# Transposing small adapter tiles on VectorE instead of TensorE in a fused residual chain

## The chip, the cores and the metric

One Trainium2 chip, one core. The time is the device time of the whole kernel in microseconds (us), from one launch. The kernel before took 558.91 us, the median of three runs (558.53 to 559.02).

## The reference

x has 64 batches of 32 channels by 512. Four layers are added to it one after the other:

```
x = x + L0(x)   # SwiGLU MLP with a low-rank adapter per batch of 32 rows
x = x + L1(x)   # 32x32 channel mixing, chosen per batch
x = x + L2(x)   # 512x512 linear plus top-2 of 8 low-rank experts
x = x + L3(x)   # 32x32 channel mixing, chosen per batch

# L0, with 16 adapters of rank 16:
t    = einsum('bri,bni->bnr', A[idx], inp)                   # 32 rows x 16
lora = base + einsum('bor,bnr->bno', B[idx], t) * 0.5
act  = silu(lora(x, gate)) * lora(x, up)                     # 512 -> 1376
down = lora(act, down)                                       # 1376 -> 512
```

The change is in L0 alone, where the small results t (for gate and up) and td (for down) must be turned so that the rank lies on the partitions before they are multiplied with B.

## The kernel before

**Tiles and steps.** The 2048 rows are 16 tiles of 128 rows, and a tile holds 4 batches. L0 works in 48 steps, ORDER (L122): three chunks of F for each tile, n = 0 (352 columns), 1 and 2 (512 each). Step s computes gate and up of its chunk, their product act, and down of the chunk two steps back. The first six steps have an order of their own, since the weights still arrive; from step 6 on step s is tile s // 3, chunk s % 3. After L0 the other layers run tile by tile. Every operand of a matmul is split into a high part in float32r and a low rest; a product is three matmuls (`product`, L1354), and where one side holds both parts stacked on the partitions, two (`stacked`, L1360).

**The adapters.** t of all four adapters of a tile is computed for all 128 rows: 128 columns, in the order batch, gate or up, rank. For n = 0 and tile 2 and later these columns are part of gate's matmuls (480 columns). A mask (`mask_t`, L1116) keeps for each row only the columns of its own batch and scales them by 0.5, so that the result is block-diagonal in batches. It writes the masked 64 columns twice (d = 0, 1), so that a 128x128 transpose on TensorE (`transpose_t`, L1401, twice, for gate and up) gives them on 128 partitions: 64 for the high part and 64 for the low one. ScalarE casts all 128 partitions (`job_hi`, kind "t", L948), and VectorE overwrites the upper 64 with the rest (`job_lo`, kind "t", L1193). The result t_hl is the stationary operand of `adapters(s)` (L1409), for all three steps of the tile. td goes the same way with one transpose: `mask_td` (L1129), `transpose_td` (L1453), kind "td", and `down_adapters` (L1457), which closes a tile's down; then "x1" adds the residual and SP stores the tile.

**The order.** ScalarE and VectorE both walk through the list `lane_jobs(s)` (L226): ScalarE does the high part of each split, VectorE the low part and the products; each waits for the other by semaphores (s_hi, s_lo), strictly in list order. After a step's jobs ScalarE also does `high_bd` (L1005), which waits for a DMA that stores an earlier block. For a tile after the third the list of n = 0 is: mask of t, act, t, gate, next b. For n = 1: act, x, bd, gate, mask of td, next b. For n = 2: td, act, x1, the next adapters' weights, gate, next b. TensorE's order is written out from L1542 on. For n = 0 it is gate, up, transpose_t, down of s - 2, adapters. For n = 2: half of gate, transpose_td, the rest of gate, half of up, down_adapters, the rest of up, adapters, down of s - 2. POOL gathers the adapters' rows with indirect DMAs; the rows of B lie in the order given by the index idx_rank, made with the mask is_rank (L102, L1101). SP's queue moves act through memory so that it lands turned: VectorE first turns act in squares of 32 by 32 within SBUF (`blocks`, L1141), which is the only use of its transpose in L0.

Of the kernel before, what the change touches and what calls it, by code (L numbers as in the profile page):

```python
# [29 lines left out]
F32 = mybir.dt.float32  # L30
# [7 lines left out]
P = 128  # L38
# [57 lines left out]
def const_array():  # L96
    p = np.arange(P)
    blocks = {

        "scale_ch": LORA_SCALE * (p[:, None] // CH == np.arange(TB)[None, :]),  # L100

        "is_rank": p[:, None] // RANK % TB == np.arange(TB)[None, :],  # L102
        "is_ch": p[:, None] // CH == np.arange(TB)[None, :],
        "row_rank": (p % RANK)[:, None],
        "row_ch": (p % CH)[:, None],
        "row": p[:, None],
        "unit_ch": p[:, None] % CH == np.arange(CH)[None, :],
        "iota": np.broadcast_to(np.arange(EXPERTS), (P, EXPERTS)),
    }
# [116 lines left out]
def lane_jobs(s):  # L226
# [38 lines left out]
def bass_conditioned_residual_chain(nc, x_t, x_rows, it_cond, it_lang, wgu, wd, a_all, a_gu, a_d, b_d,  # L265
# [6 lines left out]
    with ExitStack() as ctx:  # L272
# [59 lines left out]
        b_sel, b_raw = sb_raw("b_sel", [2, 2, 2 * H], mem_a)  # L332
        t_m = sb("t_m", [2, 2, TR], F32, mem_a)

        t_hl = sb("t_hl", [2, 2, P], F32R, mem_a)

        picked = t_m[:, 0, 0, :]
        td = sb("td", [2, TR], F32, mem_a)
        td_hl = sb("td_hl", [P], F32R, mem_a)
# [11 lines left out]
        act_t = ps("act_t", [HC, P], banks_a)  # L351
        t_ps = ps("t_ps", [HC, P], banks_a)
        banks_a.close()
# [88 lines left out]
        s_tm = sem("s_tm")  # L442
        s_tt = sem("s_tt")
        s_gu = sem("s_gu")
# [9 lines left out]
        s_tdm = sem("s_tdm")  # L454
        s_tdt = sem("s_tdt")
        s_dl = sem("s_dl")
# [110 lines left out]
        def base_cols(i):  # L567

            at = (1 - i % 2) * AD_HALF
            return down_ps[:, :, at:at + HALF]  # L570

        def td_of(i):
# [315 lines left out]
        def _(sc):  # L888
# [15 lines left out]
            def job_hi(job):  # L904
# [43 lines left out]
                elif kind == "t":  # L948
                    i = job[1]
                    sc.wait_ge(s_tt, i + 1)  # L950
                    if i >= 2:
                        sc.wait_ge(s_gu, gu_done(i - 2))
                    hi(t_hl[:, i % 2, :, :], t_ps[:, 0:2, :])
                elif kind == "td":
                    i = job[1]
                    sc.wait_ge(s_tdt, i + 1)
                    if i >= 1:
                        sc.wait_ge(s_dl, i)
                    hi(td_hl[:], t_ps[:, 2, :])
# [115 lines left out]
        def _(ve):  # L1075
# [37 lines left out]
            def lo(out_, raw, high):  # L1113
                return ve.tensor_tensor(out_, raw, high.bitcast(F32), ALU.subtract)  # L1114

            def mask_t(i):  # L1116

                ve.wait_ge(s_tx, i + 1)
                if i >= 1:
                    ve.wait_ge(s_tt, i)  # L1120
                t = t_of(i).rearrange("p (b m r) -> p m b r", m=2, r=RANK)
                for m in range(2):
                    ins = ve.tensor_tensor(
                        t_m[:, m, :, :].rearrange("p d (b r) -> p d b r", r=RANK),
                        t[:, m, :, :].unsqueeze(1).to_broadcast([P, 2, TB, RANK]),
                        const("scale_ch").unsqueeze(1).unsqueeze(3).to_broadcast([P, 2, TB, RANK]), ALU.mult)
                ins.then_inc(s_tm, 1)

            def mask_td(i):  # L1129
                ve.wait_ge(s_d, NC * (i + 1))  # L1130
                if i >= 1:
                    ve.wait_ge(s_tdt, i)
                for d in range(2):
                    ins = ve.tensor_tensor(
                        td[:, d, :].rearrange("p (j b r) -> p j b r", j=2, r=RANK),
                        td_of(i).rearrange("p j (b r) -> p j b r", r=RANK),
                        const("scale_ch").rearrange("p (j b) -> p j b", j=2).unsqueeze(3).to_broadcast(
                            [P, 2, TB // 2, RANK]), ALU.mult)
                ins.then_inc(s_tdm, 1)

# [18 lines left out]
            def job_lo(job):  # L1159
# [193 lines left out]
        def _(pe):  # L1353
# [46 lines left out]

            def transpose_t(i):  # L1401
                pe.wait_ge(s_tm, i + 1)
                if i == 0:
                    pe.wait_ge(s_ident, 16)
                for m in range(2):
                    mm = pe.transpose(t_ps[:, m, :], t_m[:, m, :, :].rearrange("p d n -> p (d n)"), ident)
                mm.then_inc(s_tt, 1)

            def adapters(s):  # L1409
# [10 lines left out]
            def transpose_act(d):  # L1420
                i, n = divmod(d, NC)
                s = step_of(i, n)
                pe.wait_ge(s_mul, s + 1)
                before = max((k for k in range(d) if k not in MOVED), default=None)
                if before is not None:
# [6 lines left out]
            def down(d):  # L1432
# [18 lines left out]
                mm.then_inc(s_d, 1)  # L1451

            def transpose_td(i):  # L1453
                pe.wait_ge(s_tdm, i + 1)
                pe.transpose(t_ps[:, 2, :], td[:].rearrange("p d n -> p (d n)"), ident).then_inc(s_tdt, 1)

# [91 lines left out]
            up(1, 0, HC // 2)  # L1548
            transpose_t(0)
            up(1, HC // 2, HC)  # L1550
# [4 lines left out]
            transpose_act(0)  # L1555
            transpose_t(1)
            whole(up, 3)
# [12 lines left out]
            gate(5, HC // 2, HC)  # L1570
            transpose_td(0)
            transpose_act(3)
# [9 lines left out]
            whole(up, 6)  # L1582
            transpose_t(2)
# [34 lines left out]
            l2_base(0, 0, 0, 1)  # L1618
            transpose_td(NT - 1)
            l1(2)  # L1620
# [94 lines left out]
```

## Time and profile before

| | |
|---|---|
| median of three runs | 558.91 us |
| time of the profiled execution | 558.51 us |
| its span, first to last instruction | 556.7 us |
| TensorE busy (matmuls) | 546.2 us, 98% |
| VectorE busy | 314.4 us, 56% |
| ScalarE busy | 210.5 us, 38% |
| POOL busy | 209.2 us, 38% |
| granted clock of TensorE | 1.00 of full speed in all slices |

Busy time is a sum over instructions, and a matmul's end is modelled and overlaps the next one's start; so the busy time of TensorE does not tell how fast it could be, and the distance between starts is the better measure of a matmul's price. Idle time of another engine costs nothing as long as TensorE doesn't wait for it.

### The profile page before, as it was taken

What the parts mean: (1) busy time and instruction counts of PE and PEld (TensorE: products, weight loads), DVE (VectorE), ACT (ScalarE), POOL (GpSimd) and SP (SyncE); (2) the same over time, 40 slices, a digit from 0 to 9 for tenths busy, and PEclk for the clock granted to TensorE, in tenths of its full rate; (3) what the DMA queues carried; (4) which work ended last, traced back from release to release, by engine and by line L of the source; (5) the groups of instructions that cost most, each with busy time, mean ns of one, the idle gap of its engine ahead of it and who ended that gap; (6) DMA issues with size and microseconds to landing.
All of it is one profiled execution on the core that took longest, in us unless ns stands there. A gap on an engine that the chain in (4) does not pass through costs nothing.

```text
span 556.7 us, 8715 instructions
## 1 busy us (share of the span) xinstructions
PE 546.2 (98%) x3172; PEld 493.2 (89%) x3172; DVE 314.4 (56%) x717; ACT 210.5 (38%) x416; POOL 209.2 (38%) x236
## 2 busy tenths in 40 slices
PE   5999999999999999999999999999999999999997
PEld 5879988898889898989898989898989899999996
DVE  6797364544464545454545454545454477777775
ACT  6675132423342424242424232323233442444442
POOL 5852144746584747332323332232322232122100
PEclk9999999999999999999999999999999999999999
DMA  8984346666666666656464645555545832676742
GB/s 289 369 252 171 114 151 207 171 205 195 197 205 203 196 210 189 206 188 192 148 190 148 183 156 185 153 182 158 179 158 175 304 97 93 195 240 211 234 145 77
DMA packets 72027, 104.68 MB, mean 188 GB/s; under 512 B 9392, under 2 KB 39728, under 8 KB 71984
## 3 DMA queue, kind: packets, MB, share of 16 engines
q1 hardware_dynamic: 60960, 66.82, 36.5%
q0 software_dynamic: 10880, 37.23, 22.3%
q8 instruction: 25, 0.41, 0.3%
q14 instruction: 18, 0.15, 0.1%
q10 hardware_dynamic: 144, 0.06, 0.1%
HBM read 77.87 MB, written 26.21 MB: 187 GB/s over the span
## 4 chain that ended last, share of the span: by engine, by line
PE 90%; DMA 5%; DVE 2%; SPq 1%; ACT 1%; issue 0%; ACTq 0%; DVEq 0%
PE gu_ps L1356 13%; PE gu_ps L1358 13%; PE gu_ps L1357 13%; PE down_ps L1356 8%; PE down_ps L1357 8%; PE down_ps L1358 8%; PE l_ps L1356 5%; PE l_ps L1357 5%; PE l_ps L1358 5%; PE gu_ps L1363 3%; PE gu_ps L1364 3%; DMA x_res<-act_blocks 1%; DMA b_sel_raw<-b_gu,idx_rank 1%; SPq L704 1%; DMA bd<-bd_hl 1%; DMA act_blocks<-act 1%
## 5 line engine op out<-in xcount | busy, mean ns | idle before, releaser
L794 POOL DMA_INDIRECT b_sel_raw<-b_gu,idx_rank x48 | 48.1, 1001 | 154.9 <-PE gu_ps L1364 144.8
L1356 PE MATMUL down_ps<-wd_sb,act_hl 128*128 128x288 f32 (+1 forms) x352 | 105.1, 299 | 0.6 <-DVE wd_sb L1114 0.3
L1357 PE MATMUL down_ps<-wd_sb,act_hl 128*128 128x288 f32 (+1 forms) x352 | 103.8, 295 | 0.0
L1358 PE MATMUL down_ps<-wd_sb,act_hl 128*128 128x288 f32 (+1 forms) x352 | 103.6, 294 | 0.0
L1356 PE MATMUL gu_ps<-w_sb,xt 128*128 128x512 f32 x256 | 102.0, 399 | 0.0
L1358 PE MATMUL gu_ps<-w_sb,xt 128*128 128x512 f32 x256 | 100.4, 392 | 0.0
L1357 PE MATMUL gu_ps<-w_sb,xt 128*128 128x512 f32 x256 | 100.3, 392 | 0.0
L794 POOL DMA_INDIRECT a_raw<-a_all,idx_batch x60 | 65.6, 1093 | 60.1 <-DVE wd_sb L1114 46.1
L1178 DVE TENSOR_TENSOR act<-act,gu_ps 128x512 f32<-128x512 f32 (+1 forms) x47 | 29.8, 634 | 98.2 <-ACT act L917 98.2
L917 ACT ACTIVATE act<-gu_ps 128x512 f32<-128x512 f32 (+1 forms) x47 | 26.1, 555 | 147.5 <-PE gu_ps L1364 147.5
L1356 PEld LDWEIGHTS down_ps<-wd_sb,act_hl 128*128 128x128 f32 (+1 forms) x352 | 66.0, 188 | 2.9 <-DVE act_hl L1114 1.0
L1357 PEld LDWEIGHTS down_ps<-wd_sb,act_hl 128*128 128x128 f32 (+1 forms) x352 | 66.1, 188 | 1.2
L1358 PEld LDWEIGHTS down_ps<-wd_sb,act_hl 128*128 128x128 f32 (+1 forms) x352 | 66.0, 188 | 0.0
L1358 PEld LDWEIGHTS gu_ps<-w_sb,xt 128*128 128x128 f32 x256 | 48.0, 188 | 10.6
L1356 PEld LDWEIGHTS gu_ps<-w_sb,xt 128*128 128x128 f32 x256 | 48.1, 188 | 9.4
L1357 PEld LDWEIGHTS gu_ps<-w_sb,xt 128*128 128x128 f32 x256 | 48.2, 188 | 8.2
L1114 DVE TENSOR_TENSOR b_sel<-b_sel_raw,b_sel 128x1024 fp32r<-128x1024 f32 (+1 forms) x48 | 52.3, 1090 | 1.3 <-ACT b_sel L897 1.2
L858 POOL TENSOR_TENSOR x_hl<-x,x_hl 128x512 fp32r<-128x512 f32 x16 | 21.6, 1353 | 69.8 <-ACT x_hl L1021 69.8
L897 ACT CAST b_sel<-b_sel_raw 128x1024 fp32r<-128x1024 f32 (+1 forms) x48 | 45.7, 953 | 1.4 <-DMA b_sel_raw<-b_gu,idx_rank 1.1
L1356 PE MATMUL l_ps<-w2ra_hl,x2t_hl 128*128 128x328 f32 (+1 forms) x128 | 41.6, 325 | 0.0
L1357 PE MATMUL l_ps<-w2ra_hl,x2t_hl 128*128 128x328 f32 (+1 forms) x128 | 39.7, 311 | 0.0
L1358 PE MATMUL l_ps<-w2ra_hl,x2t_hl 128*128 128x328 f32 (+1 forms) x128 | 39.5, 309 | 0.0
(160 smaller groups left out, 1054.5 us busy)
## 6 DMA issues: line engine op xcount, KB each, us to landing
act_blocks<-act SPq DMA_DIRECT2D x39, 256.0 KB, 4.0
x_res<-act_blocks SPq DMA_DIRECT2D x156, 64.0 KB
xt_raw<-x_t SPq DMA_DIRECT2D x16, 256.0 KB, 4.9
w_sb_raw<-wgu SPq DMA_DIRECT2D x16, 256.0 KB, 8.0
x_res<-x_rows SPq DMA_DIRECT2D x16, 256.0 KB, 2.8
x_after_l<-x_res SPq DMA_DIRECT2D x16, 256.0 KB, 2.0
bd<-bd_hl SPq DMA_DIRECT2D x16, 256.0 KB, 2.3
x<-x_after_l SPq DMA_DIRECT2D x16, 256.0 KB, 2.8
```

Source lines behind the costliest of these rows:

```text
L704: sp.dma_start(x_res[j * CH:(j + 1) * CH, 1, :].rearrange("f (b n) -> f b n", b=TB), act_scratch[d % 2, :, j * P:(j + 1) * P].rearrange("( ...
L794: nc.gpsimd.indirect_dma_start(out=dst, out_offset=None, in_=table, in_offset=bass.IndirectOffsetOnAxis(ap=idx, axis=0)).then_inc(s, 16)
L858: pool.tensor_tensor(x1_hl[:, t % 2, 1, :], x1[:, t % 2, :], x1_hl[:, t % 2, 0, :].bitcast(F32), ALU.subtract).then_inc(s_x1lo, 1)
L897: sc.copy(out_, in_).then_inc(s_hi, 1)
L917: sc.activation(act_of(s), gate_of(s), ACT.Silu).then_inc(s_silu, 1)
L1114: return ve.tensor_tensor(out_, raw, high.bitcast(F32), ALU.subtract)
L1178: ve.tensor_tensor(a, a, up_of(s), ALU.mult).then_inc(s_mul, 1)
L1356: pe.matmul(out_, stationary[0], moving[0], start=start, stop=False, skip_group_check=True)
L1357: pe.matmul(out_, stationary[0], moving[1], start=False, stop=False, skip_group_check=True)
L1358: return pe.matmul(out_, stationary[1], moving[0], start=False, stop=stop, skip_group_check=True)
L1363: pe.matmul(out_, stationary, moving[0], start=False, stop=False, skip_group_check=True)
L1364: return pe.matmul(out_, stationary, moving[1], start=False, stop=True, skip_group_check=True)
```

## The change

TensorE no longer transposes t and td. The mask writes its columns once. The high part is cast by ScalarE from the masked tile in SBUF into t_rows, with high and low side by side (batch, part, rank: 32 columns for each batch); VectorE subtracts the low part, transposes the 128 columns in squares of 32 by 32, and copies the result into t_hl. Since the masked tile is block-diagonal in squares of 32, the squares on the diagonal are the whole transpose and the others are zero. The partitions of t_hl are now in the order batch, part, rank, so the rows of B are gathered by the mask is_ch. VectorE waits for each of its own results (`turn`) before it uses it. The tile t_m is shared by t and td, and the squares of t are put into t_m and the used part of t_rows. td's split ("td") moves in the list from the start of step n = 2 to the end of step n = 1, from tile 3 on.

```
     if n == 1:
         x = [("x", i + 1, 0)] if i + 1 < NT else []
-        return acts + x + [("bd", i - 1), ("gate", s), ("tdm", i - 1), ("b", s + 1)]
-    jobs = [("td", i - 1)] + acts[:1] + [("x1", i - 1)] + acts[1:] if i > 2 else acts
+        return acts + x + [("bd", i - 1), ("gate", s), ("tdm", i - 1), ("b", s + 1), ("td", i - 1)]
+    jobs = acts[:1] + [("x1", i - 1)] + acts[1:] if i > 2 else acts
...
                 elif kind == "t":
                     i = job[1]
-                    sc.wait_ge(s_tt, i + 1)
-                    if i >= 2:
-                        sc.wait_ge(s_gu, gu_done(i - 2))
-                    hi(t_hl[:, i % 2, :, :], t_ps[:, 0:2, :])
+                    sc.wait_ge(s_tm, i + 1)
+                    if i >= 1:
+                        sc.wait_ge(s_lo, s_lo_of(("t", i - 1)))
+                    hi(t_rows[:, :, :, 0, :], masked_t())
...
-                pick(0, "is_rank", TB)
+                pick(0, "is_ch", TB)
...
+            def turn(ins):
+
+                turned[0] += 1
+                ins.then_inc(s_turn, 1)
+                ve.wait_ge(s_turn, turned[0])
+
+            def transposed(out_, in_):
+                return ve.transpose(out_, in_.bitcast(F32).rearrange("p b d r -> p (b d r)"))
...
                 elif kind == "t":
-                    own = t_hl[TR:, job[1] % 2, :, :]
-                    ins = lo(own, t_ps[TR:, 0:2, :], own)
+                    i = job[1]
+                    masked.append(job)
+                    turn(lo(t_rows[:, :, :, 1, :], masked_t(), t_rows[:, :, :, 0, :]))
+
+                    parts_f32 = [t_m[:], t_rows[:, 0, :, :, :].bitcast(F32).rearrange("p b d r -> p (b d r)")]
+                    for m in range(2):
+                        turn(transposed(parts_f32[m], t_rows[:, m, :, :, :]))
+                    if i >= 2:
+                        ve.wait_ge(s_gu, gu_done(i - 2))
+                    for m in range(2):
+                        ins = ve.tensor_copy(t_hl[:, i % 2, m, :], parts_f32[m])
                 elif kind == "td":
-                    ins = lo(td_hl[TR:, :], t_ps[TR:, 2, :], td_hl[TR:, :])
+                    i = job[1]
+                    masked.append(job)
+                    turn(lo(td_rows[:, :, 1, :], masked_td(), td_rows[:, :, 0, :]))
+                    turn(transposed(t_m[:], td_rows[:]))
+                    if i >= 1:
+                        ve.wait_ge(s_dl, i)
+                    ins = ve.tensor_copy(td_hl[:], t_m[:])
...
-            transpose_td(0)
...
                 gate(s, 0, HC // 2)
-                if finishes:
-                    transpose_td(i - 1)
                 gate(s, HC // 2, HC)
...
-                if n == 0:
-                    transpose_t(i)
-                else:
+                if n > 0:
                     adapters(s)
```

## Rows read from the trace of the kernel before

**Rows 1.** The page, its first lines: busy us, share of the span, instructions.

```profile
span 556.7 us, 8715 instructions
...
PE 546.2 (98%) x3172; PEld 493.2 (89%) x3172; DVE 314.4 (56%) x717; ACT 210.5 (38%) x416; POOL 209.2 (38%) x236
```

**Rows 2.** Groups by form: count | busy us, mean ns | idle us before them.

```profile
L1406 PE MATMUL t_ps<-ident_sb,t_m 128*128 128x128 f32 x32 | 6.1, 272 | 0.0
...
L1123 DVE TENSOR_TENSOR t_m<-gu_ps,head_sb 128x128 f32<-128x128 f32 x30 | 7.3, 286 | 18.4 <-PE gu_ps L1358 18.4
...
L1151 DVE STREAM_TRANSPOSE act<-act 128x256 f32<-128x256 f32 x13 | 5.8, 445 | 0.4
...
L1155 DVE STREAM_TRANSPOSE act<-act 128x96 f32<-128x96 f32 x13 | 3.1, 236 | 0.0
...
L1306 DVE TENSOR_SCALAR lang<-lang 128x128 f32<-128x128 f32 x1 | 0.2, 227 | 0.0
...
L1253 DVE RECIPROCAL route<-route 128x1 f32<-128x1 f32 x16 | 2.6, 164 | 0.5
...
L1109 DVE TENSOR_SCALAR idx_ch<-sel,head_sb 128x16 uint32<-128x16 f32 x1 | 0.2, 234 | 0.0
```

**Rows 3.** Timeline of TensorE around a transpose of td: start us, us, instruction.

```profile
164.98 0.39 PE L1358 MATMUL gu_ps<-w_sb,xt 128*128 128x512 f32 x1
...
165.56 0.40 PE L1357 MATMUL gu_ps<-w_sb,xt 128*128 128x512 f32 x1
```

**Rows 4.** Timeline around the transposes of t in step 15.

```profile
176.50 0.68 DVE L1114 TENSOR_TENSOR act_hl<-x_res,act_hl 128x512 fp32r<-128x512 f32 x1
...
177.66 0.32 PE L1358 MATMUL gu_ps<-wu_sb,xt 128*128 128x352 f32 x1
...
178.17 0.30 PE L1357 MATMUL down_ps<-wd_sb,act_hl 128*128 128x288 f32 x1
...
181.24 0.32 PE L1363 MATMUL gu_ps<-b_sel,t_hl 128*128 128x352 f32 x1
```

**Rows 5.** Timeline of the start-up; in brackets idle time before and its end.

```profile
8.21 1.16 POOL L794 DMA_INDIRECT a_raw<-a_gu,idx_batch  x1 [0.30 <-issue]
...
8.98 0.39 DVE L1102 TENSOR_SCALAR idx_rank<-sel,head_sb 128x16 uint32<-128x16 f32 x1
...
22.21 0.94 POOL L794 DMA_INDIRECT a_raw<-a_d,idx_batch  x1 [0.31 <-issue]
22.25 0.43 DVE L1114 TENSOR_TENSOR t_hl<-t_ps,t_hl 64x256 fp32r<-64x256 f32 x1
...
22.82 0.40 PE L1363 MATMUL gu_ps<-b_sel,t_hl 128*128 128x352 f32 x1
...
31.04 0.43 DVE L1114 TENSOR_TENSOR t_hl<-t_ps,t_hl 64x256 fp32r<-64x256 f32 x1
...
31.57 0.89 DVE L1114 TENSOR_TENSOR b_sel<-b_sel_raw,b_sel 128x704 fp32r<-128x704 f32 x1
...
33.69 1.64 POOL L794 DMA_INDIRECT b_sel_raw<-b_gu,idx_rank  x1 [4.62 <-PE down_ps L1364]
...
37.41 0.37 PE L1356 MATMUL down_ps<-wd_sb,act_hl 128*128 128x288 f32 x1 [0.28 <-DVE wd_sb L1114]
```

**Rows 6.** Timeline around the down adapters of tile 2.

```profile
136.03 1.22 DVE L1114 TENSOR_TENSOR b_sel<-b_sel_raw,b_sel 128x1024 fp32r<-128x1024 f32 x1
...
139.52 0.41 ACT L1010 CAST bd_hl<-bd_raw 128x256 fp32r<-128x256 f32 x1 [5.44 <-DMA bd<-bd_hl]
139.58 0.39 PE L1358 MATMUL gu_ps<-w_sb,xt 128*128 128x512 f32 x1
...
140.47 0.39 PE L1363 MATMUL down_ps<-bd_hl,td_hl 128*128 128x256 f32 x1 [0.50 <-DVE td_hl L1114]
```

**Rows 7.** Timeline of TensorE at the down of step 7.

```profile
94.46 0.40 PE L1356 MATMUL down_ps<-wd_sb,act_hl 128*128 128x288 f32 x1 [0.23 <-DVE act_hl L1114]
```

More of the change, by code:

```diff
@@ L332, in bass_conditioned_residual_chain @@
         b_sel, b_raw = sb_raw("b_sel", [2, 2, 2 * H], mem_a)
-        t_m = sb("t_m", [2, 2, TR], F32, mem_a)
+        t_m = sb("t_m", [2 * TR], F32, mem_a)
+        t_rows = sb("t_rows", [2, TB, 2, RANK], F32R, mem_a)
+        td_rows = sb("td_rows", [TB, 2, RANK], F32R, mem_a)
         t_hl = sb("t_hl", [2, 2, P], F32R, mem_a)
-        picked = t_m[:, 0, 0, :]
-        td = sb("td", [2, TR], F32, mem_a)
+        picked = t_rows[:, 0, :, :, :].bitcast(F32).rearrange("p b d r -> p (b d r)")[:, 0:BATCHES]
         td_hl = sb("td_hl", [P], F32R, mem_a)
@@ L351, in bass_conditioned_residual_chain @@
         act_t = ps("act_t", [HC, P], banks_a)
-        t_ps = ps("t_ps", [HC, P], banks_a)
+        spare_ps = ps("spare_ps", [HC, P], banks_a)
         banks_a.close()
@@ L442, in bass_conditioned_residual_chain @@
         s_tm = sem("s_tm")
-        s_tt = sem("s_tt")
+        s_turn = sem("s_turn")
         s_gu = sem("s_gu")
@@ L454, in bass_conditioned_residual_chain @@
         s_tdm = sem("s_tdm")
-        s_tdt = sem("s_tdt")
         s_dl = sem("s_dl")
@@ L570, in base_cols, with masked_t, masked_td @@
             return down_ps[:, :, at:at + HALF]
+        def masked_t():
+            return t_m[:].rearrange("p (m b r) -> p m b r", m=2, r=RANK)
+        def masked_td():
+            return t_m[:, 0:TR].rearrange("p (b r) -> p b r", r=RANK)
         def td_of(i):
@@ L949, in job_hi @@
                     i = job[1]
-                    sc.wait_ge(s_tt, i + 1)
-                    if i >= 2:
-                        sc.wait_ge(s_gu, gu_done(i - 2))
-                    hi(t_hl[:, i % 2, :, :], t_ps[:, 0:2, :])
+                    sc.wait_ge(s_tm, i + 1)
+                    if i >= 1:
+                        sc.wait_ge(s_lo, s_lo_of(("t", i - 1)))
+                    hi(t_rows[:, :, :, 0, :], masked_t())
                 elif kind == "td":
                     i = job[1]
-                    sc.wait_ge(s_tdt, i + 1)
+                    sc.wait_ge(s_tdm, i + 1)
                     if i >= 1:
-                        sc.wait_ge(s_dl, i)
-                    hi(td_hl[:], t_ps[:, 2, :])
+                        sc.wait_ge(s_lo, s_lo_of(("td", i - 1)))
+                    hi(td_rows[:, :, 0, :], masked_td())
                 else:
@@ L1114, in lo, with t_m_free @@
                 return ve.tensor_tensor(out_, raw, high.bitcast(F32), ALU.subtract)
+            masked = []
+            def t_m_free():
+                if masked:
+                    ve.wait_ge(s_lo, s_lo_of(masked[-1]))
             def mask_t(i):
                 ve.wait_ge(s_tx, i + 1)
[L1119 to L1126, printed above, removed]
@@ L1127, in mask_t @@
-                ins.then_inc(s_tm, 1)
+                t_m_free()
+                ve.tensor_tensor(masked_t(), t_of(i).rearrange("p (b m r) -> p m b r", m=2, r=RANK),
+                                 const("scale_ch").unsqueeze(1).unsqueeze(3).to_broadcast([P, 2, TB, RANK]),
+                                 ALU.mult).then_inc(s_tm, 1)
             def mask_td(i):
                 ve.wait_ge(s_d, NC * (i + 1))
[L1131 to L1138, printed above, removed]
@@ L1139, in mask_td @@
-                ins.then_inc(s_tdm, 1)
+                t_m_free()
+                ve.tensor_tensor(masked_td().rearrange("p (j b) r -> p j b r", j=2),
+                                 td_of(i).rearrange("p j (b r) -> p j b r", r=RANK),
+                                 const("scale_ch").rearrange("p (j b) -> p j b", j=2).unsqueeze(3).to_broadcast(
+                                     [P, 2, TB // 2, RANK]), ALU.mult).then_inc(s_tdm, 1)
+            turned = [0]
+            def turn(ins):
+                turned[0] += 1
+                ins.then_inc(s_turn, 1)
+                ve.wait_ge(s_turn, turned[0])
@@ L1399, in up @@
                     product(up_of(s), x_of(i, c), wgu_parts(n, 1, c)[1:], c == 0, False)
[L1401 to L1407, printed above, removed]
             def adapters(s):
@@ L1423, in transpose_act @@
                 pe.wait_ge(s_mul, s + 1)
+                if d == 0:
+                    pe.wait_ge(s_ident, 16)
                 before = max((k for k in range(d) if k not in MOVED), default=None)
@@ L1451, in down @@
                 mm.then_inc(s_d, 1)
-            def transpose_td(i):
-                pe.wait_ge(s_tdm, i + 1)
-                pe.transpose(t_ps[:, 2, :], td[:].rearrange("p d n -> p (d n)"), ident).then_inc(s_tdt, 1)
             def down_adapters(i):
@@ L1548, in _ @@
             up(1, 0, HC // 2)
-            transpose_t(0)
             up(1, HC // 2, HC)
@@ L1555, in _ @@
             transpose_act(0)
-            transpose_t(1)
             whole(up, 3)
@@ L1582, in _ @@
             whole(up, 6)
-            transpose_t(2)
             down(5)
@@ L1618, in _ @@
             l2_base(0, 0, 0, 1)
-            transpose_td(NT - 1)
             l1(2)
```

1 line of the change is left out of this document (removed).

## The prediction

> **What bounds the kernel now.** I read the page first. TensorE is busy 546.2 of 556.7 us and VectorE 314.4 [rows 1], so outside a few places an instruction less on TensorE is time less on the clock, and an instruction more on VectorE costs nothing until its result is late. Then I read the groups by form, for what each operation costs; the timeline of TensorE around the transposes, for what each is worth there; the waits and the timeline of the first 38 us and around 94 and 140 us, where TensorE stands still. The profiled execution took 558.51 us, 0.40 under the median of 558.91.
>
> **Removed from TensorE.** 32 transposes of t_m [rows 2] and 16 of td, one a tile. The row says 272 ns each, but matmuls overlap, so the row is not the price. The price is in the starts. Matmuls of 512 columns follow each other every 0.23 us. Around a td transpose the starts run 164.98, then 165.56 two matmuls later [rows 3]: 0.58 less 2 x 0.23 leaves 0.12 us. Around a pair for t, from the last 352-column matmul at 177.66 to the second 288-column one at 178.17, there are 0.51 us [rows 4]; the two ordinary steps of 0.16 and 0.13 leave 0.22 us. That is 0.11 to 0.12 us for each transpose. The Trainium skill ("TensorE: Matmul & The Clock Gate", Part 4) gives about 275 ns for one in a kernel's context; its figure agrees with the 272 ns of the row, not with the spacing of starts. By its figure as an estimate the 48 would be worth 13.2 us.
>
> Two pairs (tiles 0 and 1) lie before 37.4 us, where TensorE ends up waiting for VectorE anyway, and count in the start-up below. The pair of tile 3 lies just ahead of a wait: the matmul at 94.46 waits for act_hl [rows 7], at the end of a chain of transfers that begins with x1 of tile 1 and not with TensorE's pace in between; that pair only lengthens the wait. So 13 pairs x 0.22 = 2.9 and 16 x 0.12 = 1.9: **-4.8 us**.
>
> **Added on VectorE.** For t: one mask for two (286 ns each [rows 2]), a subtraction of 128 columns (the same 286 as nearest row), two block transposes of 128 columns, two copies of 128 columns. The trace has block transposes of 96 columns at 236 and of 256 at 445 ns [rows 2]; by interpolation 128 columns are 280. A copy within SBUF is not shown; the nearest is the one-source operation on 128x128 at 227 ns (L1306), the lower bound is that of a tiny operation, 164 ns, the upper the 286 of the mask. A wait on its own result costs little: L1253 stands idle 0.5 us in 16, some 30 ns each [rows 2]. After the high half, t needs 0.29 + 2 x 0.28 + 2 x 0.23 + 3 x 0.03 = 1.4 us (1.3 to 1.5) where the old low half took 0.43. td needs 0.2 + 0.28 + 0.23 + 0.06 = 0.8 where it took 0.3. ScalarE's casts get a little shorter.
>
> Is that hidden? In the steady state ScalarE takes the high half as soon as the mask is done, no longer when up has ended. VectorE ends act's low half at 176.50 + 0.68 = 177.2, so t_hl is ready at 178.6. TensorE wants it at 181.24 [rows 4], or 181.0 with the pair gone: the 3.2 us of down(s-2) cover it with 2.4 to spare. Hidden, 14 times. For td the split now lies behind b(s+1) in step n = 1 on both queues. What is behind it there: ScalarE's high_bd and VectorE's act of the next step, each kept waiting at most until the mask of td, which comes when down(s-2) ends. Near 140 us b's low half runs from 136.03 for 1.22 us [rows 6], so td_hl is done at 138.1, and down_adapters wants it at 139.8. In tile 1 the split stays in step 7, directly ahead of its use; there the cover is thinnest, and what that may cost is in the first rival. No DMA is moved; SP and POOL keep their order, and the moved split only lets act(s-2) be split earlier in steps with n = 2.
>
> **A stall that goes.** The matmul before down_adapters(2) starts at 139.58 and could be followed at 139.81; it is followed at 140.47, so 0.66 us are lost. ScalarE's cast of td stood behind high_bd, which began only at 139.52 after its DMA [rows 6]. In the changed order the cast of td comes ahead of high_bd. What is late next is act(9), cast at 139.52 + 0.41 = 139.9, and its down comes only at the end of the step: **-0.66 us**, or nothing if another wait is there.
>
> **The start-up pays.** VectorE is loaded here. Before, it began the low half of t(0) at 22.25 directly behind b(1), and adapters(0) began at 22.82 [rows 5]; with the pair gone TensorE would be there at 22.5. Now the chain of 1.4 us begins at 22.1 (one mask less) and ends at 23.5 to 23.6: adapters(0) is 0.8 late. It decides little, since VectorE's own order sets the next wait. There: one mask less (0.2), then t(1) takes 1.4 instead of the 0.53 from 31.04 to 31.57, so b(2)'s low half moves from 31.57 to 32.25 [rows 5], and from there to down(0) at 37.41 VectorE has no gap. TensorE resumes 0.7 us later: **+0.7 us**, between 0.4 (copies at 164 ns, gaps in VectorE that I can't see taking some) and 1.5.
>
> The upper end is a mechanism that the trace hints at. L1102 took 389 ns at 8.98, L1109 of the same form 234 [rows 2, 5]; a gather ran on POOL from 8.21 for 1.16 us, and both end at 9.37. So an operation of one source within SBUF may have to wait for a POOL gather under way. The copies of t(0) fall on the gather at 22.21 (0.94 us) [rows 5] and the one behind it; if the second copy loses, it waits for nearly one more such gather, and adapters(0) starts after 24.4, which delays silu(0), the product and all of VectorE's order. The Trainium skill ("SBUF — State Buffer", the box on "DVE blocks DMA") says that an fp32 copy within SBUF locks GpSimd out of the ports it writes descriptors with, and the other way about, whoever comes first. L1102 agrees. In the steady state such a wait adds up to 1 us to 1.4 us, within the 2.4 to spare.
>
> **Sum.** -4.8 - 0.66 + 0.7 = -4.8 us; 558.51 - 4.8 = 553.7 as a profiled execution, 554.1 as a median.
>
> **Rivals.**
> *The stall near 140 us stays or another takes its place* (act(9) or x1(2) late there, or td(1) late in step 7): no gain of 0.66, 554.8. Chance 0.12.
> *The start-up costs double* by copies that wait for gathers, or by VectorE's saturation going on past the first down: +1.5 instead of 0.7, with some lost later, 555 to 556. Chance 0.15. For it: L1102. Against: POOL stands idle for the 4.6 us before 33.69 [rows 5], when t(1) is copied.
> *The transposes were nearly free*, because the start stamps of the matmuls beside them are modelled: gain about zero, start-up paid, 558.5 to 559.2. Against it: both kinds give the same 0.11. Chance 0.04.
> *TensorE is held for the whole 272 ns*: 44 x 0.27 = 12 us less, 547. That is also where the skill's 275 ns leads. The starts speak against it; chance 0.02.
> *Slower:* t_hl comes late at adapters of every step n = 0. This needs the chain on VectorE to grow from 1.4 beyond 3.8 us, as when each of the three waits on its own result costs 1 us and not 0.03: then 14 x 0.6 = 8 us of stall, and 4 us are lost net, 562. Chance 0.03. A milder mix, in which td's split blocks the ScalarE queue and lets silu or act wait, could cost 0.3 us a tile, 558.8: chance 0.03.
>
> **How the numbers follow.** The forecast has 0.61: by its own terms 553.4 to 554.9 (transposes 0.11 or 0.12, start-up 0.4 to 1.5). With the first two rivals that is 0.88. The range goes from 553.0 to 556.4, and it covers what the median of a few runs may stand off the profiled execution. What a measurement here can tell from no change is 0.2%, 1.1 us. Faster by more holds the forecast, the first two rivals and the 547: 0.90. Within it: nearly-free transposes and the mild mix, 0.05. Slower: 0.05.
>
> **What would show it.** TensorE has 48 instructions less (3172 becomes 3124), and the starts of 512-column matmuls run on at 0.23 us where td's transpose was. VectorE is busy about 327 us (16 x 0.8 more). Block transposes of 128 columns near 280 ns, copies near 230, some longer where a gather runs. adapters(0) begins near 23.6, down(0) near 38.1. The stall before down_adapters(2) is gone, the one near 94 us is 0.2 longer. TensorE waits for t_hl in tile 0 alone. The prediction is wrong if TensorE's waits name t_hl or td_hl in the steady state, if the start-up loses over 2 us, or if a tile of three steps in the steady state shortens by other than 0.34 us (0.22 + 0.12).

## The result, and the profile after

The changed kernel took 553.66 us, the median of six runs (552.26 to 554.27), beside 559.38 us (558.53 to 560.80, six runs) for the kernel before on the same chip: a ratio of 0.9897, with a 95% interval of 0.9879 to 0.9916. The forecast was 554.1 us in a range of 553.0 to 556.4. The profiled execution of the changed kernel took 554.27 us.

The page of the changed kernel, its first lines, answers to [rows 1]:

```profile
span 552.4 us, 8713 instructions
...
PE 539.1 (98%) x3124; PEld 487.8 (88%) x3124; DVE 330.7 (60%) x781; ACT 209.2 (38%) x416; POOL 212.7 (38%) x236
```

TensorE has the 48 instructions less, 3124 of 3172. VectorE has 64 more and is busy 16.3 us longer, at 330.7 (327 was forecast), and the span is 4.3 us shorter. The work that was added is larger than the time that was won, and it is on the engine with idle time.

The groups by form of the changed kernel, those that the change brought (count | busy us, mean ns | idle us before them):

```profile
L1121 DVE TENSOR_TENSOR td_rows<-t_m,td_rows 128x64 fp32r<-128x64 f32 x16 | 5.4, 338 | 0.6 <-ACT td_rows L904 0.6
...
L1155 DVE STREAM_TRANSPOSE t_m<-t_rows 128x128 f32<-128x128 f32 x16 | 5.0, 313 | 0.6
...
L1155 DVE STREAM_TRANSPOSE t_m<-td_rows 128x128 f32<-128x128 f32 x16 | 5.0, 312 | 0.5
L1220 DVE CAST t_hl<-t_rows 128x128 fp32r<-128x128 f32 x16 | 4.9, 304 | 0.0
```

The block transpose of 128 columns is 312 ns and not the interpolated 280. The idle 0.5 or 0.6 us before each group of 16 are the waits on VectorE's own results, some 35 ns each. The means of 338 and 304 ns are drawn up by a few long ones; the view of the tile t_hl shows it by minimum, median and maximum in ns, and the first and last start:

```profile
L1220 DVE CAST t_hl<-t_m x16: 226/227/764, 22.8 to 422.3; 128x128 fp32r<-128x128 f32 x16
L1220 DVE CAST t_hl<-t_rows x16: 213/220/454, 22.9 to 422.5; 128x128 fp32r<-128x128 f32 x16
```

The timeline of the changed kernel in a steady tile, with the first matmul of its adapters:

```profile
420.53 0.29 DVE L1134 TENSOR_TENSOR t_m<-gu_ps,head_sb 128x128 f32<-128x128 f32 x1 [1.27 <-PE gu_ps L1389]
...
421.33 0.28 DVE L1121 TENSOR_TENSOR t_rows<-t_m,t_rows 128x128 fp32r<-128x128 f32 x1
...
422.49 0.22 DVE L1220 CAST t_hl<-t_rows 128x128 fp32r<-128x128 f32 x1
...
425.41 0.33 PE L1394 MATMUL gu_ps<-b_sel,t_hl 128*128 128x352 f32 x1
```

From the subtraction at 421.33 to the end of the last copy at 422.71 the chain takes 1.38 us (1.4 was forecast). TensorE comes for t_hl at 425.41, so 2.7 us of cover are left (2.4 forecast). The waits of TensorE in the changed kernel, behind the 5.7 us before its first matmul (us in total, times, longest):

```profile
PE down_ps L1387 <- DVE act_hl L1121: 1.5, 2, 0.8
PE gu_ps L1394 <- DVE t_hl L1220: 1.3, 1, 1.3
PE down_ps L1394 <- DVE b_sel L1121: 1.3, 1, 1.3
```

t_hl is waited for once, in the start-up, and td_hl never. The two waits for act_hl are at down of steps 6 and 7, near 88 and 96 us. The timeline of the start-up of the changed kernel answers to [rows 5]:

```profile
23.27 0.40 PE L1394 MATMUL gu_ps<-b_sel,t_hl 128*128 128x352 f32 x1 [1.33 <-DVE t_hl L1220]
...
32.02 0.78 ACT L904 CAST b_sel<-b_sel_raw 128x704 fp32r<-128x704 f32 x1 [2.51 <-DMA b_sel_raw<-b_gu,idx_rank]
32.14 0.22 DVE L1220 CAST t_hl<-t_rows 128x128 fp32r<-128x128 f32 x1
...
32.83 0.89 DVE L1121 TENSOR_TENSOR b_sel<-b_sel_raw,b_sel 128x704 fp32r<-128x704 f32 x1 [0.47 <-ACT b_sel L904]
...
38.66 0.37 PE L1387 MATMUL down_ps<-wd_sb,act_hl 128*128 128x288 f32 x1 [0.28 <-DVE wd_sb L1121]
```

**Where the time went.** Take each matmul's start in the changed kernel minus that of the same matmul before; that is how far the changed kernel is behind (+) or ahead (-):

| matmul, start before | offset, us |
|---|---|
| adapters(0), 22.82 | +0.45 |
| down(0), 37.41 | +1.25 |
| first down adapters after down(0), 55.35 | +1.13 |
| down(6), 86.84 | +1.22 |
| down(7), 94.46 | +1.62 |
| down adapters, 140.47 | +0.42 |
| down adapters, 168.11 | -0.10 |
| down adapters, 444.61 | -4.06 |
| Layer 2, 523.19 | -4.31 |

The changed kernel is behind by 0.7 to 1.6 us from 33 to 137 us, gets 0.84 back at one place near 140 us, the price of td's transpose in it, and then wins 0.40 us in each of the ten tiles from 168 to 445 us: 0.16 to 0.19 where a transpose of td stood and 0.22 where a pair for t did.

The transpose of td of before stood between 164.98 and 165.56 [rows 3]. The timeline of TensorE in the changed kernel at the same place of a tile:

```profile
219.61 0.40 PE L1387 MATMUL gu_ps<-w_sb,xt 128*128 128x512 f32 x1
219.85 0.39 PE L1388 MATMUL gu_ps<-w_sb,xt 128*128 128x512 f32 x1
220.08 0.40 PE L1389 MATMUL gu_ps<-w_sb,xt 128*128 128x512 f32 x1
```

The starts run on at 0.23 us. Three labels of the rows and of the prediction are to be put right: the tile whose down adapters are at 140.47 is tile 3 and not 2, in step 14; the act that is cast behind high_bd there is that of step 12 and not 9; and the step of [rows 4] is 18 and not 15. No term of the sum hangs on them.

### The profile page after: what moved, and what is told of

Read it like the earlier page. It is cut to its first block, busy times and chain, and to the rows that moved or that the text cites. A ratio compares the mean times of both kernels' runs of the same rounds, so it can differ in the third digit from the quotient of the medians.

```text
span 552.4 us, 8713 instructions
## 1 busy us (share of the span) xinstructions
PE 539.1 (98%) x3124; PEld 487.8 (88%) x3124; DVE 330.7 (60%) x781; ACT 209.2 (38%) x416; POOL 212.7 (38%) x236
## 4 chain that ended last, share of the span: by engine, by line
PE 89%; DMA 5%; DVE 3%; ACT 1%; POOL 1%; issue 1%; SPq 0%; DVEq 0%; ACTq 0%
PE gu_ps L1387 13%; PE gu_ps L1389 13%; PE gu_ps L1388 13%; PE down_ps L1387 8%; PE down_ps L1388 8%; PE down_ps L1389 8%; PE l_ps L1387 5%; PE l_ps L1388 5%; PE l_ps L1389 5%; PE gu_ps L1394 3%; PE gu_ps L1395 3%; DMA b_sel_raw<-b_gu,idx_rank 3%; DMA x_res<-act_blocks 2%; DVE b_sel L1121 1%; POOL a_raw L801 1%; PE down_ps L1395 1%
## 5 line engine op out<-in xcount | busy, mean ns | idle before, releaser
L801 POOL DMA_INDIRECT a_raw<-a_all,idx_batch x60 | 70.5, 1175 | 59.9 <-DVE wd_sb L1121 45.9
```

The costliest lines, as they stand in the source:

```text
L801: nc.gpsimd.indirect_dma_start(out=dst, out_offset=None, in_=table, in_offset=bass.IndirectOffsetOnAxis(ap=idx, axis=0)).then_inc(s, 16)
```

## The experiments

**The changed kernel again (no edit).**

> The changed kernel once more, unchanged. It is the yardstick for the others of this call and shows what differs from one execution to the next. The first profile had the start-up's wait end when the gather of b for step 2 landed (its cast on ScalarE at 32.0 us, 30.8 before the change) and not when VectorE was done with t(1) (32.4). If that landing is chance, the time at which the first down starts (38.66 in the first profile) moves by some tenths of a us here; if VectorE's added work sets it (my prediction's term, down(0) at 38.1), it stays within 0.1 and follows the end of t(1)'s copies directly. Median 553.7, between 552.5 and 554.5.

It took 553.37 us (552.94 to 553.68, four runs), ratio 0.9887 (0.985 to 0.9925); its profiled execution took 553.26. The timeline of its start-up:

```profile
30.48 0.78 ACT L904 CAST b_sel<-b_sel_raw 128x704 fp32r<-128x704 f32 x1 [1.05 <-DMA b_sel_raw<-b_gu,idx_rank]
30.92 0.28 DVE L1121 TENSOR_TENSOR t_rows<-t_m,t_rows 128x128 fp32r<-128x128 f32 x1
...
32.21 0.88 DVE L1121 TENSOR_TENSOR b_sel<-b_sel_raw,b_sel 128x704 fp32r<-128x704 f32 x1
...
37.99 0.37 PE L1387 MATMUL down_ps<-wd_sb,act_hl 128*128 128x288 f32 x1 [0.27 <-DVE wd_sb L1121]
```

Here b(2) was cast at 30.48 and not at 32.02, and its low half ran directly behind t(1)'s chain, at 32.21 (32.25 forecast). down(0) began at 37.99, that is 0.58 behind before (0.7 forecast). So the other 0.67 us in the first profile go with the late landing of a gather of b's rows, for which ScalarE had waited 2.51 us; in a third execution (below) the cast was at 30.69 and down(0) at 38.04, so it is not there each time. In this execution down(6) and down(7) stood at +0.40 and +0.65. The timeline there:

```profile
86.08 0.51 ACT L904 CAST act_hl<-x_res 128x384 fp32r<-128x384 f32 x1 [4.06 <-DMA x_res<-act_blocks]
...
87.24 0.40 PE L1387 MATMUL down_ps<-wd_sb,act_hl 128*128 128x288 f32 x1 [0.44 <-DVE act_hl L1121]
...
93.71 0.62 ACT L904 CAST act_hl<-x_res 128x512 fp32r<-128x512 f32 x1 [4.66 <-DMA x_res<-act_blocks]
...
95.11 0.40 PE L1387 MATMUL down_ps<-wd_sb,act_hl 128*128 128x288 f32 x1 [0.70 <-DVE act_hl L1121]
```

TensorE waits for act's split, and the split for the transfer that brings act back. Before, the two casts were at 85.69 and 93.06, and a row shows TensorE waiting only behind the second (0.23 us [rows 7]).

**Before, with td's split moved and nothing else** (the first two replaced lines of the change).

> The kernel before with only td's split moved to the end of step n = 1; TensorE keeps its 48 transposes. Theory: the cast of td then stands ahead of high_bd, so the stall of 0.66 us before down_adapters(2) goes and the time is 0.6 to 0.8 us less than before (ratio 0.9987). ScalarE now waits for TensorE's transpose with high_bd and act behind it, which has cover in steps of 10 us. Rival: the move has no effect by itself, 0 us; second rival: the blocked ScalarE queue costs 0.2 us a tile, 3 us more than before.

It took 559.78 us (557.96 to 560.86, twelve runs), ratio 0.9999 (0.998 to 1.0018). An effect of 0.66 us would be 0.12% and lies within that interval; only the trace can show it. The timeline around the down adapters of tile 3 answers to [rows 6]:

```profile
137.90 0.29 DVE L1114 TENSOR_TENSOR td_hl<-t_ps,td_hl 64x128 fp32r<-64x128 f32 x1 [0.29 <-ACT td_hl L897]
139.17 0.41 ACT L1010 CAST bd_hl<-bd_raw 128x256 fp32r<-128x256 f32 x1 [1.30 <-DMA bd<-bd_hl]
...
140.17 0.28 PE L1363 MATMUL down_ps<-bd_hl,td_hl 128*128 128x256 f32 x1
```

td_hl is ready at 138.2, before high_bd's cast at 139.17, and the matmul waits for nothing; TensorE's offset to before falls by 0.70 us there. That the move did it is not shown, though. In [rows 6] the matmul came 0.95 us behind the start of high_bd's cast (139.52 to 140.47). Here that cast began at 139.17, 0.35 earlier, so in the old order the matmul could have started at 140.12; it started at 140.17, where TensorE came to it. The cast's earlier start alone would have ended this stall. What the kernel's time gains from the move, this run doesn't resolve.

**The changed kernel with td's split back at the head of step n = 2** (the same two lines the other way about).

> The changed kernel with td's split back at the head of step n = 2. Theory: the stall before down_adapters(2) comes back, 0.66 us and some 0.4 more since VectorE's chain behind the late cast is now 0.8 us and not 0.3: 0.8 to 1.2 us more than the changed kernel; in the other tiles VectorE's work at the head of the step is hidden. Rival: act's split is now behind td in 13 tiles and its transfer late, 2 us or more lost. Second rival: the move was worth nothing, the same time as the changed kernel.

It took 554.68 us (553.26 to 556.18, six runs), ratio 0.991 (0.9879 to 0.9941): 1.3 us above the changed kernel's 553.37, with ranges that overlap (0.8 to 1.2 was expected). The stall near 140 us was small, 0.4 us. Instead there was a larger one 56 us later; the timeline there:

```profile
194.61 0.41 ACT L1017 CAST bd_hl<-bd_raw 128x256 fp32r<-128x256 f32 x1 [4.79 <-DMA bd<-bd_hl]
194.92 0.24 ACT L904 CAST td_rows<-t_m 128x64 fp32r<-128x64 f32 x1
...
195.19 0.71 DVE L1121 TENSOR_TENSOR td_rows<-t_m,td_rows 128x64 fp32r<-128x64 f32 x1 [2.35 <-ACT td_rows L904]
...
196.28 0.37 DVE L1228 CAST td_hl<-t_m 128x128 fp32r<-128x128 f32 x1
...
196.71 0.39 PE L1394 MATMUL down_ps<-bd_hl,td_hl 128*128 128x256 f32 x1 [1.17 <-DVE td_hl L1228]
```

Read from the bottom: TensorE waits for the copy, VectorE for ScalarE's cast, and the cast stands behind high_bd, which waited 4.79 us for its DMA. So the stall belongs to whichever tile's DMA lands late, not to tile 3. With the longer chain on VectorE the matmul comes 2.1 us behind the start of high_bd's cast (194.61 to 196.71) and not 0.95, so the old place of td is dearer in the changed kernel than it was before. In the first profile of the changed kernel high_bd's cast began at 193.83 and the down adapters of that tile at 195.23, 1.4 us later and without a wait; an estimate from these rows is that the old place would have cost some 0.7 us there. The move does not remove a fixed 0.66 us; it avoids a wait whose place and size vary from one execution to the next.

**The changed kernel with 44 idle transposes on TensorE, where the old ones stood** (all but the pairs of tiles 0 and 1; they turn the identity into a tile that nobody reads, so nothing waits for them).

```
+            def idle_transposes(n):
+                for m in range(n):
+                    pe.transpose(spare_ps[:, m, :], ident, ident)
...
                 gate(s, 0, HC // 2)
+                if finishes:
+                    idle_transposes(1)
...
-                if n > 0:
+                if n == 0:
+                    idle_transposes(2)
+                else:
                     adapters(s)
```

> The changed kernel with 44 transposes put back on TensorE at their old places (28 for t from tile 2 on, 16 for td), of the identity into a bank that nobody reads: TensorE's price alone, with no one waiting for it. Theory: 0.11 to 0.12 us each as the starts of before suggest, less the pair of tile 3 that a wait hides: 4.8 us more than the changed kernel, 558.5. The tile period should be 0.40 us longer, as it was before. Rivals: nearly free (0 to 1 us), since the starts are modelled; or 272 ns each as their rows say, 12 us.

It took 559.10 us (558.10 to 560.07, ten runs), ratio 0.9988 (0.9964 to 1.0012): all of the gain is gone. The view of the tile spare_ps:

```profile
L1480 PE MATMUL spare_ps<-ident_sb x44: 270/271/273, 54.3 to 460.6; 128*128 128x128 f32 x44
```

559.10 less 553.37 is 5.7 us, 0.13 us for each of the 44; by the two spans (556.2 and 551.5) it is 4.7 us, 0.11 each. A tile then takes what it took before: the offset to before is -0.54 at 333.5 us and -0.58 at 444.6. The row shows 271 ns for each. The price in this stream of matmuls is less than half of the row. Beside the kernel before, of the whole change only 0.13 us of the medians is left (559.23 less 559.10), so nearly all of its gain is TensorE's time.

**A longer chain for t on VectorE: 5 or 10 more block transposes in tiles 2 to 15**, each waited for, so 1.7 and 3.45 us more.

```
                     for m in range(2):
-                        turn(transposed(parts_f32[m], t_rows[:, m, :, :, :]))
+                        for again in range(6 if m == 0 and i >= 2 else 1):
+                            turn(transposed(parts_f32[m], t_rows[:, m, :, :, :]))
```

> The changed kernel, the first block transpose of t done six times and not once for tiles 2 to 15 (same result, 5 x 0.35 = 1.7 us more on VectorE's chain to t_hl). Theory: t_hl is ready 2.6 to 2.7 us before adapters wants it in the steady state (422.7 against 425.4 in the profile of the changed kernel), so nothing is lost: 553.7, no wait of TensorE on t_hl. VectorE's busy time rises by 23 us to 354. Rival: VectorE's load itself costs (products and act's splits late), 0.2 us a tile, 3 us more.

> The same with eleven times, 3.45 us more chain. Theory: now t_hl is late by 3.45 - 2.7 = 0.75 us in each of 14 tiles, a bit more where copies wait for POOL: 10 to 13 us more, 564 to 567, and TensorE's waits name t_hl. Rival: the cover is larger than the profile shows and nothing is lost; or VectorE as a whole becomes the bound, 20 us and more.

On the chip of these two runs TensorE stood still in the start-up, at a place where the profiles above have no such wait: for 5.43 us before 26.49 with 5 more, for 4.17 before 26.56 with 10 more, and for 5.65 before 26.37 in the kernel before (last experiment). Behind it the granted clock was 0.50 of full speed, that is 1.2 GHz, until about 32, 38 and 28 us in the three. The kernel before took 564.89 us there (560.37 to 568.45, and one of 17 executions 1921.86), so the ratios are less sure. With 5 more it took 560.36 us (558.96 to 563.96, ten runs), ratio 0.9939 (0.9908 to 0.997). With 10 more it took 577.42 us (575.09 to 577.83, four runs), ratio 1.0214 (1.0156 to 1.0273). TensorE's waits for t_hl, first with 5 more, then with 10 more:

```profile
PE gu_ps L1395 <- DVE t_hl L1221: 1.2, 3, 0.9
```

```profile
PE gu_ps L1395 <- DVE t_hl L1221: 13.0, 15, 1.4
```

Beside the changed kernel's second profile, the one with 1.7 us more has two short waits in the steady state, 0.17 us each, at each of which TensorE falls back by 0.41 or 0.42 us, and none in the other tiles. None was expected. With 3.45 us more, every adapters(s) of n = 0 waits from tile 2 on; the row of the wait says 0.75 or 0.76 us in late tiles, as expected, but TensorE falls back by 0.97 to 1.01 us a tile. The row counts from the modelled end of the matmul before, not from where the next could have started, so it understates the loss by some 0.24 us. That, and the start-up, is why the kernel lost more than the expected 10 to 13 us: from 55 to 445 us alone the trace shows 15.8. At the wanting matmul itself the delay is 0.91 us; 3.45 less 0.91 is 2.5, and the cover read in the trace was 2.7. The slower rival's mechanism is real, and its threshold lies about where the rows put it, near 3.8 us for the chain; the chain is at 1.38.

**A longer chain in tile 1 alone** (the same edit with `i == 1`, 1.7 us), on another chip, beside the changed kernel once more.

> The changed kernel a third time, as the yardstick of this call. 1.0% under the kernel before, down(0) at 38.0 to 38.7.

> The changed kernel with five more block transposes in the chain of tile 1 alone (1.7 us more on VectorE in the start-up, nothing elsewhere). Theory: from the end of t(1) to the first down VectorE has no gap, so down(0) comes 1.7 us later than in the changed kernel and so does the end, but for what the two waits on act's transfer near 88 and 96 us take back (those chains begin after it, so nothing): 1.5 to 1.7 us more. Rival: the gather of b for step 2 sets the start-up, then the first 0.5 to 1 us are free.

The unchanged kernel took 553.77 us (553.62 to 553.88, four runs), ratio 0.9897 (0.9881 to 0.9914). With the longer chain in tile 1 it took 556.32 us (555.03 to 559.08, ten runs), ratio 0.9943 (0.9926 to 0.9961), 2.5 us more. The timeline with the longer chain:

```profile
30.60 2.04 DVE L1155 STREAM_TRANSPOSE t_m<-t_rows 128x128 f32<-128x128 f32 x6
...
33.30 0.88 DVE L1121 TENSOR_TENSOR b_sel<-b_sel_raw,b_sel 128x704 fp32r<-128x704 f32 x1
...
34.24 0.43 PE L1395 MATMUL down_ps<-b_sel,t_hl 128*128 128x352 f32 x1 [1.90 <-DVE b_sel L1121]
```

In the unchanged kernel beside it b(2)'s low half ran at 32.26 and adapters(2) began at 33.20: both are 1.04 us later here. The chain began at 30.28 and not at 30.97, which took the other 0.7 of the 1.7. At 467 us TensorE is 1.3 us behind. One chain of 1.7 us in the start-up costs over 1 us; the same chain in 14 steady tiles cost 0.83 at its waits in the trace. The median lost more than the trace, and the granted clock goes with it: the two executions whose mean clock was 1.000, the profiled one among them, took 555.09 and 555.03 us, and the eight at 0.994 to 0.999 took 555.59 to 559.08. None of the eight was profiled, so where the clock fell in them is open; that it was behind a longer wait in the start-up, as in the profiles above, is likely and not shown.

**t of tiles 0 and 1 turned by TensorE after all**, from t_rows, with one copy on ScalarE (job "tc") instead of VectorE's two transposes and two copies, and t(0) ahead of b(1). The core of the edit:

```
-                0: (... ("tm", 0), w1u[3], ("b", 1), ("t", 0),
+                0: (... ("tm", 0), w1u[3], ("t", 0), ("b", 1), ("tc", 0),
...
-                2: [("b", 2), ("adt", 0), ("b", 3), ("adt", 1), ...
+                2: [("b", 2), ("tc", 1), ("adt", 0), ("b", 3), ("adt", 1), ...
...
+                if kind == "tc":
+                    i = job[1]
+                    sc.wait_ge(s_tt, i + 1)
+                    sc.copy(t_hl[:, i, :, :], spare_ps[:, 0:2, :]).then_inc(s_tc, 1)
```

> The changed kernel with tiles 0 and 1 on TensorE again in a form that is cheap for VectorE: it masks and subtracts once, TensorE transposes t_rows twice, ScalarE copies the result from PSUM into t_hl; t(0) is split ahead of b(1). VectorE saves some 1.1 us for each of the two tiles in the start-up. Theory: b(2)'s low half begins at 31.3 and not 32.2, down(0) at 37.1 (38.0 in the repeated profile) and the wait for t_hl at 23.3 goes; 0.9 us less than the changed kernel, 552.8. Rival: the landing of b's gather (cast at 30.5 to 32.0) sets the start-up instead, then 0 to 0.5 us are gained.

> The version with tiles 0 and 1 transposed by TensorE out of t_rows and copied by ScalarE, beside the changed kernel on the same chip. On the first chip both engines stood still in the start-up for reasons of their own (VectorE waited 1.2 us before the mask of tile 0, TensorE 1.7 us before its first transpose), so it told nothing. Theory: VectorE's order sets down(0), and it has 0.9 us less: ratio to the changed kernel 0.9984, down(0) at 37.1. Rival: the landing of b's gather or ScalarE's added work sets it, no gain.

The first time, on the chip whose start-up stood still, it took 558.96 us (554.85 to 560.62, six runs), ratio 0.9896 (0.9847 to 0.9945), which tells nothing about a microsecond. The second time it took 553.45 us (552.45 to 554.0, four runs), ratio 0.9887 (0.9867 to 0.9907), against 553.77 for the changed kernel beside it. The timeline of the second:

```profile
32.58 0.43 PE L1407 MATMUL down_ps<-b_sel,t_hl 128*128 128x352 f32 x1
...
33.08 1.05 ACT L906 CAST b_sel<-b_sel_raw 128x1024 fp32r<-128x1024 f32 x1
...
34.17 1.23 DVE L1129 TENSOR_TENSOR b_sel<-b_sel_raw,b_sel 128x1024 fp32r<-128x1024 f32 x1
...
35.45 0.50 PE L1407 MATMUL gu_ps<-b_sel,t_hl 128*128 128x512 f32 x1 [0.56 <-DVE b_sel L1129]
```

adapters(2) begins at 32.58, 0.62 earlier than in the unchanged kernel. But the copy that ScalarE now does pushes its cast of b(3) from 32.15 to 33.08, VectorE's low half follows at 34.17, and adapters(3) waits 0.56 for it; down(0) begins at 38.28 where the unchanged kernel has 38.04. The load went from one full queue to the next. Down(0) at 37.1 and a gain of 0.9 us had been expected; neither came, and the 0.3 us between the medians lies within their spread.

**The kernel before once more, on the chip of the chains.**

> The kernel before once more, for a second profile of its start-up: down(0) at 37.4 as in the first, within 0.3; the cast of b for step 2 at 30.8 within 0.5; stall before down_adapters(2) of 0.66 us again if it is of the order of work, gone or other if it is chance of the transfer that high_bd waits for.

One run, 565.99 us. TensorE waited 5.65 us for t_m in the start-up, at a place where the first profile of before had no such wait, so this run said nothing on the question of down(0). It does answer the other question, on the stall near 140 us:

```profile
144.73 0.41 ACT L1010 CAST bd_hl<-bd_raw 128x256 fp32r<-128x256 f32 x1 [5.04 <-DMA bd<-bd_hl]
...
165.34 0.41 ACT L1010 CAST bd_hl<-bd_raw 128x256 fp32r<-128x256 f32 x1 [4.25 <-DMA bd<-bd_hl]
...
167.15 0.40 PE L1356 MATMUL down_ps<-wd_sb,act_hl 128*128 128x288 f32 x1 [1.11 <-DVE act_hl L1114]
```

The down adapters of tile 3 began at 145.68, 0.95 us behind high_bd's cast as before, and TensorE's offset to the first profile fell by 0.40 us there: most of the stall was gone with no edit at all. Twenty us later high_bd's cast was late in another step, act's split stood behind it, and TensorE waited 1.11 us, which the first profile does not have.

## Why the prediction was right, point by point

**Removed from TensorE, -4.8.** Right in mechanism, small in size. The pair for t costs 0.22 as read. td's transpose costs 0.16 to 0.19 and not 0.12, so that a tile shortens by 0.40 us and not 0.34. The prediction had named another figure than 0.34 as a sign that it is wrong, and by that sign this price was. The reading from [rows 3] took 2 x 0.23 from a distance rounded to 0.01 us; two stamps at one place are a thin base for a price of a tenth. From down(7) on the first profile shows 1.62 + 4.31 = 5.93 us won. By the prediction's terms it would be 12 pairs x 0.22 + 14 x 0.12 + 0.66 = 5.0; with 0.17 for td it is 5.7. The idle transposes show that nothing but TensorE's time is behind it. The rivals "nearly free" and "held for 272 ns" are both excluded by them: 44 cost 5.7 us, not 0 and not 12. The Trainium skill ("TensorE: Matmul & The Clock Gate", Part 4) gives some 275 ns for a transpose (128x128, bf16) in a kernel's context; the row of 271 ns agrees, for f32 here, the cost of 0.11 to 0.13 us in this dense stream doesn't.

**The stall, -0.66.** Right in its number, by luck. The changed kernel passes the place 0.84 ahead, td's 0.17 in it. But its high_bd cast began at 138.64 and the matmul at 140.89, 2.25 us later; that is more than the 0.95 of before and the 2.1 of the run with td's split put back, so there would have been no stall in the old order either. The same holds for the move alone. The step was put as a fixed stall near 140 us, and the runs show a chance: 0.40 of it gone in the second profile of before, with 1.1 us lost at 167; 0.4 and 1.2 near 196 with the split put back in the changed kernel. On the median the move alone showed nothing (0.9999). That the stall comes from a queue behind high_bd's DMA is right; that the change takes it away is made likely by the two stalls with the split put back, and shown by no pair of traces in which only the order differs.

**The start-up, +0.7.** Right: 0.58 at down(0) in the second execution and 0.63 in the third, with b(2)'s low half within 0.04 us of the forecast. The first profile has 1.25, within the forecast 0.4 to 1.5, but for a reason that the range didn't name, a gather that landed late; there the range held by luck. The reason that it did name, copies waiting for gathers, was not at work there: adapters(0) began at 23.27 and not after 24.4, since the copy of t(0) at 22.76 ran 0.23 us beside a gather.

**What was left out: the waits at down(6) and down(7).** This is the term that was mis-sized. The prediction had the wait near 94 us grow by 0.2 (tile 3's pair) and counted what TensorE wins between 37 and 87 us (td of tiles 0 and 1, the pair of tile 2: 0.46 us by its prices). Hardly any of it is left behind 95 us. In the second execution the offset goes from +0.58 at 37 us to +0.08 at 77.5, and then up to +0.40 at down(6) and +0.65 at down(7): VectorE's split behind the transfer of act sets both, so whatever TensorE had gained there it waits off. That loss, 0.65 - (0.7 - 0.46) = 0.41 us, was made good by td's higher price (14 x 0.05 = 0.7 us), so that the total came out near the forecast for two reasons that cancel, which is luck. By spans, 556.7 less 551.5 is 5.2 us, and less 552.4 is 4.3; the forecast of 4.8 lies between. By medians the gain is more, 5.7, 5.9 and 5.7 us in the three times that the two kernels were measured side by side. The median of the kernel before was 559.2 to 559.5 there, 0.7 to 1.0 above the execution that was profiled; what those executions lose has no trace.

**Added on VectorE, hidden.** Right: no wait for t_hl or td_hl in the steady state, and the chains lengthened on purpose put the limit about where the rows had it.

**The chances.** The rivals that come out within what can't be told from no change have 0.04 and 0.03, together 0.07, and the slower one 0.03; the prediction sums them up as 0.05 and 0.05. The 0.90 for faster stands.

## What to carry to other kernels

A transpose that feeds TensorE costs TensorE what the distance between the starts beside it says, here 0.11 to 0.19 us, and not the duration in its row; take that distance at several places before trusting its second digit. Where the operand is block-diagonal in squares of 32, the block transpose within SBUF is the whole transpose, and 1.4 us on an idle engine is a good price for 0.22 us on the full one, as long as the result is wanted later than it is ready. Before counting a gain, walk forward to the next place where the bounding engine waits for something else: what is won before that place can be waited off there, and of what is added in a start-up where the other engine is full most is paid (1.3 of 1.7 us here). A stall behind a DMA that one trace shows need not be there in the next: look for it in a second profile before putting its whole length into the sum.

## What the runs showed of the hardware

**A copy within SBUF can be held up by a gather on POOL.** The timeline of VectorE and POOL in the changed kernel, in two neighbouring tiles:

```profile
340.47 0.95 POOL L801 DMA_INDIRECT bd_hl_raw<-b_d,idx_rank  x1 [0.30 <-issue]
340.88 0.23 DVE L1220 CAST t_hl<-t_m 128x128 fp32r<-128x128 f32 x1
341.02 0.45 DVE L1220 CAST t_hl<-t_rows 128x128 fp32r<-128x128 f32 x1
...
368.15 0.22 DVE L1220 CAST t_hl<-t_rows 128x128 fp32r<-128x128 f32 x1
368.20 0.99 POOL L801 DMA_INDIRECT bd_hl_raw<-b_d,idx_rank  x1 [0.30 <-issue]
```

The gather ends at 341.42 and the second copy at 341.47. It is the same in five tiles in which the gather was under way (the copies at 123.67, 178.01, 286.68, 341.02 and 395.36): 0.45 us instead of 0.22, ended 0.05 after the gather. In a sixth the first copy, at 232.20, took 0.76 us and ended 0.21 after the gather. Where the copy came first, it took 0.22 and the gather 0.98 or 0.99 instead of 0.95. So each can wait for the other, but not in all of the gather: the first copy at 340.88, inside it as well, took its 0.23. The Trainium skill ("SBUF — State Buffer", the box on "DVE blocks DMA") says that GpSimd can't write descriptors while such a copy runs, and further on ("Who interferes with whom") that whoever issues first holds the shared ports for its whole instruction. The second copies agree, with 0.23 us as the price and not the whole gather that the prediction had feared; the first copies, begun and ended inside a gather, don't.

**A small subtraction of two SBUF operands can take six times its time beside a POOL operation.** The view of the tile td_rows gives its minimum, median and maximum, and the timeline the longest:

```profile
L1121 DVE TENSOR_TENSOR td_rows<-t_m,td_rows x16: 216/219/1319, 54.7 to 457.2; 128x64 fp32r<-128x64 f32 x16
```

```profile
437.25 1.41 POOL L865 TENSOR_TENSOR x_hl<-x,x_hl 128x512 fp32r<-128x512 f32 x1 [1.71 <-ACT x_hl L1028]
437.42 1.32 DVE L1121 TENSOR_TENSOR td_rows<-t_m,td_rows 128x64 fp32r<-128x64 f32 x1
```

POOL's operation ends at 438.66 and VectorE's at 438.74. The Trainium skill ("SBUF — State Buffer", "Who interferes with whom") says that a VectorE instruction with two SBUF inputs contends with a GpSimd instruction that reads SBUF; this row agrees, 219 ns having become 1319. Here it fell into idle time. td_hl was ready at 439.35 and the down adapters began at 440.55. The copies and subtractions of this change bear such hits because their results are wanted later (t_hl 2.7 us later), not because they are spared them.
